# A graph layer on one core: where W_self's first rows are loaded, and in what order its first products run

## The chip, the cores and the metric

The kernel runs on one core of a Trainium2 chip. The metric is the device time of one execution in microseconds; lower is better. The core has five engines that run their own instruction streams and meet only at semaphores: TensorE (PE in the profile), VectorE (DVE), ScalarE (ACT), GpSimd (POOL) and SyncE (SP). Loads and stores are DMAs, which SP and ACT issue here.

## The reference

The inputs are 625 nodes of 512 features, 20625 edges with four relations and a weight each, and the weights of the layer. Cut to what matters:

```
h   = relu(layernorm(x))
agg = segment_sum over edges of (h[src] @ W_rel[type] + b_rel[type]) * weight   # by dst
agg = agg / max(sum of the weights by dst, 1)
x1  = layernorm(h + h @ W_self + b_self + agg) * g1 + b1
ffn = gelu(x1 @ W1 + b_ffn1) @ W2 + b_ffn2
out = x + layernorm(x1 + ffn) * g2 + b2
```

The change touches only the first lines: the normalized rows h and their product with W_self (512 x 512).

## The kernel before

The 625 nodes are five row tiles of 125 rows, numbered 0 to 4 (in the trace all of them are `x`, in the built program `x_60`). All float32 products are made of three products of a rounded part ("high", type fp32r) and what is left ("low"): high by high, low by high and high by low. Each operand must therefore be split: ScalarE casts the high part, then VectorE subtracts it from the original to get the low part.

The start of the program, tile by tile, is a relay between three engines:

- `row_mean(c)` on VectorE waits for tile c of x, takes its statistics and writes the negated mean (lines 629, 633, 634).
- `h_of(c)` on ScalarE subtracts the mean and clamps at zero (line 506). The scale of the layer norm is applied later.
- `turn_h(c)` on TensorE transposes the tile in four pieces (line 1033).
- `hT_high(c)` on ScalarE casts the transposed tile's high part (line 511), and `hT_low(c)` on VectorE makes its low part (line 638).

W_self comes as two units of 256 rows; a unit is two halves of 128 rows (k = 0 and 1). Unit 0's halves are two DMAs of 256 KB with signals of their own. `first_high(0)` and `first_high(1)` (lines 498 and 501) cast them, and two subtractions (lines 651 and 656) make their low parts; the signals are `first_hi` and `w_hi`, `first_lo` and `w_lo`. Unit 1 is one DMA of 512 KB, split by `high_part(1)` (line 492, ScalarE) and `low_part(1)` (line 625, VectorE).

On TensorE `first_product(k, s)` multiplies row tile s by half k of unit 0, high by high and low by high; `product_lo` adds high by low; `unit_product(u, s)` is all six products of unit u and tile s. Ten and then three dummy products of ones, 128 x 128 each, fill time before the first real product.

Nothing schedules this at run time. Every engine takes its instructions strictly in the order in which the code of that engine is written, so an instruction that waits holds back all that stand behind it. The order of SP's DMAs is also that of the code: three tiles of x (112 of each tile's rows; ScalarE's queue loads the 13 rows that are left over), then W_self's two first halves, then two tiles of x, unit 1, the edge lists, and the rest. After the self product come the four relations' products (units 2 to 9), the products that pick the edges' fields (`pick`), the building of the adjacency blocks and their products, and the two feed-forward layers.

Of the kernel before, what the change touches and what calls it, by code (L numbers as in the profile page):

```python
# [19 lines left out]
def gnn_layer(nc, x, src, dst, etype, ew, W_self, b_self, W_rel, b_rel, ln1_g, ln1_b, ln2_g, ln2_b,  # L20
# [156 lines left out]
    with ctx:  # L177
# [112 lines left out]
        def stage_view(u):  # L290
            v = stage[u % STAGES][:, :]
            return v if U_REL <= u < U_W1 else v.rearrange("p (k n) -> p k n", k=2)
# [59 lines left out]
        @block.sync  # L352
        def _(sp):

            def load_x(c):
                p0, p1 = SPANS[0]
                sp.dma_start(x1[p0:p1, c, :], x[c * TN + p0:c * TN + p1, :]).then_inc(x_in[c], 16)  # L357

            def load(u):
                if u >= STAGES:  # L360
                    sp.wait_ge(w_lo, u - STAGES + 1)
                sp.dma_start(stage_view(u), units[u][0]).then_inc(stage_in[u % STAGES], 16)

            def sums_by_relation(c):

                sp.wait_ge(A_a, group_of(c, NG - 1))
                sp.wait_ge(A_b, group_of(c, NG - 1))
                if c >= 2:
                    sp.wait_ge(agg_ps, c - 1)
                for row, half in zip(SUM_ROWS, (0, 1, 0)):  # L370
                    sp.dma_start(f32(sums[row:row + TR, c % 2, :]),
                                 f32(AT[c % 2][half][SUMS:SUMS + 1, :, :])).then_inc(sums_in[c % 2], 16)

            for c in range(3):
                load_x(c)
            sp.dma_start(stage_view(0)[:, 0, :], units[0][0][:, 0, :]).then_inc(first_in, 16)
            sp.dma_start(stage_view(0)[:, 1, :], units[0][0][:, 1, :]).then_inc(stage_in[0], 16)
            for c in range(3, NT):
                load_x(c)
            load(1)  # L380
            sp.wait_ge(tails, 1)
            for f, vec, signal in ((1, dst, dst_in), (3, ew.bitcast(I32), w_in), (0, src, src_in), (2, etype, src_in)):
                flat = vec.rearrange("(p e) -> p e", p=TN)
                sp.dma_start(raw[0:TN, f, 0:EC], flat).then_inc(signal, 16)
                sp.dma_start(raw[0:TN - 1, f, EC:EW], flat[1:TN, 0:EW - EC]).then_inc(signal, 16)
            load(2)
            for buf, vec in ((bself_bc, b_self), (g1_bc, ln1_g), (b1_bc, ln1_b)):
                row = vec.rearrange("(a d) -> a d", a=1)
                sp.dma_start(buf[:, :], row.broadcast_to([P, D])).then_inc(consts_in, 16)
            with nc.allow_non_contiguous_dma("bias by partition"):  # L390
                sp.dma_start(bf1, b1.rearrange("(f p) -> p f", p=P)).then_inc(consts_in, 16)
            sp.wait_ge(blk_iotas, 3)
            for row in SUM_ROWS:
                for r in range(R):
                    sp.dma_start(brel_raw[row + r * NT:row + (r + 1) * NT, :],
                                 b_rel[r:r + 1, :].broadcast_to([NT, D])).then_inc(brel_in, 16)
            for u in range(STAGES, U_REL):
                load(u)
            sums_by_relation(0)
            for u in range(U_REL, U_REL + STAGES):  # L400
                load(u)
            for c in range(1, NT):
                sums_by_relation(c)
            for u in range(U_REL + STAGES, NU):
                load(u)

            sp.wait_ge(agg_ps, NT)
            for c in range(NT):
                for p0, p1 in SPANS:
                    sp.dma_start(x_again[p0:p1, c, :], x[c * TN + p0:c * TN + p1, :]).then_inc(late_in, 16)  # L410
            for buf, vec in ((g2_bc, ln2_g), (b2_bc, ln2_b), (bf2_bc, b2)):
                row = vec.rearrange("(a d) -> a d", a=1)
                sp.dma_start(buf[:, :], row.broadcast_to([P, D])).then_inc(late_in, 16)
            for c in range(NT - 1):
                sp.wait_ge(y_out, c + 1)
                for p0, p1 in SPANS:
                    sp.dma_start(out[c * TN + p0:c * TN + p1, :], ybuf[p0:p1, c % 2, :]).then_inc(out_done[c % 2], 16)
            p0, p1 = SPANS[0]
            for i, (d0, d1) in enumerate(HALVES):
                sp.wait_ge(y_out, NT + i)  # L420
                sp.dma_start(out[(NT - 1) * TN + p0:(NT - 1) * TN + p1, d0:d1],
                             ybuf[p0:p1, (NT - 1) % 2, d0:d1]).then_inc(last_done, 16)
            for i in range(2):
                sp.wait_ge(out_done[i], ROWS_IN * len(range(i, NT - 1, 2)))
            sp.wait_ge(last_done, 16 * 2 * len(HALVES))
# [52 lines left out]
        def _(act):  # L478
# [24 lines left out]
            def h_of(c):  # L503

                act.wait_ge(xmean, c + 1)
                a.activation(x1[0:TN, c, :], x1[0:TN, c, :], ACT.Relu,
                             bias=nm[0:TN, c:c + 1]).then_inc(h_act, 1)

            def hT_high(c):
                act.wait_ge(hT_ps, c + 1)  # L510
                a.copy(hT_all[:, :, 0, :, c, :],
                       h_bank(c).rearrange("p (h k m) -> p h k m", h=2, k=2)[:, :, :, 0:TN]).then_inc(hT_a, 1)
# [25 lines left out]
            a.activation(nm1, ones[:, 0:1], ACT.Relu).then_inc(table_in, 1)  # L538

            h_of(0)  # L540
            h_of(1)
            hT_high(0)
            first_high(0)
            hT_high(1)
            first_high(1)
            h_of(2)
            hT_high(2)
            h_of(3)
            hT_high(3)
            h_of(4)  # L550
            hT_high(4)
            high_part(1)
            act.wait_ge(dst_in, 16 * 2)
            a.copy(DF[0:TN, 1, 0:EW], raw[0:TN, 1, :]).then_inc(dsts, 1)
            high_part(2)
# [58 lines left out]
        def _(dve):  # L614
# [21 lines left out]
            def hT_low(c):  # L636
# [8 lines left out]

            row_mean(0)
            row_mean(1)
            row_mean(2)
            hT_low(0)
            dve.wait_ge(first_hi, 1)  # L650
            v.tensor_tensor(units[0][2][:, 0, :], stage_view(0)[:, 0, :], f32(units[0][1][:, 0, :]),
                            ALU.subtract).then_inc(first_lo, 1)
            hT_low(1)
            row_mean(3)
            dve.wait_ge(w_hi, 1)
            v.tensor_tensor(units[0][2][:, 1, :], stage_view(0)[:, 1, :], f32(units[0][1][:, 1, :]),
                            ALU.subtract).then_inc(w_lo, 1)
            hT_low(2)
            row_mean(4)
            hT_low(3)  # L660
            hT_low(4)
            dve.wait_ge(dst_in, 16 * 2)
            link(v.tensor_copy(edge_d, raw[0:TN, 1, 0:ES * (EG + 1)].rearrange("p (j e) -> p j e", e=ES)[:, :, 0]))
# [1 line left out]
            dve.wait_ge(w_in, 16 * 2)  # L665
            v.tensor_reduce(wmax, raw[0:TN, 3, 0:EC].bitcast(F32), AX.X, ALU.max,
                            apply_absolute_value=True).then_inc(wmax_in, 1)
            low_part(1)
            dve.wait_ge(iotas, 1)
            for j in range(EG + 1):  # L670
                i = v.tensor_scalar(ahead[0:TN, j, :], slot_d[0:TN, :], edge_d[:, j:j + 1], None, ALU.is_gt)
# [352 lines left out]
        def _(pe):  # L1024
# [30 lines left out]
            def product_lo(u, s):  # L1055

                half, w = u % 2, wring[:, u % WRING, :, :, :]
                if s == 0:
                    pe.wait_ge(w_lo, u + 1)
                if s == 0 and u == 0:  # L1060
                    pe.wait_ge(first_lo, 1)
                for k in range(2):
                    i = mm(ps[0:TN, s, :], hT_all[:, half, 0, k, s, :], w[:, 1, k, :], False, half == 1 and k == 1)
                return i

            def unit_product(u, s):
                product_hi(u, s)
                return product_lo(u, s)

            def first_product(k, s):  # L1070

                if s == 0 and k == 0:
                    pe.wait_ge(first_hi, 1)
                if s == 0 and k == 1:
                    pe.wait_ge(w_hi, 1)
                if k == 0:
                    pe.wait_ge(hT_a, s + 1)
                mm(ps[0:TN, s, :], hT_all[:, 0, 0, k, s, :], wring[:, 0, 0, k, :], k == 0)
                if k == 0:
                    pe.wait_ge(hT_b, s + 1)  # L1080
                mm(ps[0:TN, s, :], hT_all[:, 0, 1, k, s, :], wring[:, 0, 0, k, :], False)
# [89 lines left out]
            dummies(WARM[0])  # L1171
            pe.wait_ge(blk_iotas, 2)
            turn_h(0)
            turn_h(1)
            dummies(WARM[1])
            first_product(0, 0)
            first_product(1, 0)
            turn_h(2)
            first_product(0, 1)
            first_product(1, 1)  # L1180
            product_lo(0, 0)
            turn_h(3)
            product_lo(0, 1)
            unit_product(0, 2)
            turn_h(4)
            unit_product(0, 3)
            unit_product(0, 4).then_inc(unit_done, 1)
            unit_product(1, 0).then_inc(self_ps, 1)
            unit_product(1, 1).then_inc(self_ps, 1)

            pe.wait_ge(wmax_in, 1)
            mm(WSUM, ones[0:TN, :], wmax, True, True).then_inc(wsum_ps, 1)
# [169 lines left out]
```

## Time and profile before

| | |
|---|---|
| median of 3 timed runs | 242.24 us (242.18 to 242.71) |
| the profiled execution | 242.38 us |
| its span in the trace | 240.6 us |
| PE busy | 232.5 us, 97% of the span |
| DVE busy | 180.8 us, 75% |
| ACT busy | 65.7 us, 27% |
| PE busy from 5.33 to 8.85 us | 2.58 of 3.52 us |
| PE busy from 8.85 to 14.34 us | 5.49 of 5.49 us |

TensorE is busy nearly all the time; what it isn't lies mostly ahead of 8.85 us and behind 235 us. A time that is lost or won at the start is therefore lost or won at the end, unless something between holds TensorE up.

### The profile page before, as it was taken

To read this page: it belongs to the slowest core of one execution; us is meant where nothing else is said; L and a number is where in the kernel's file an instruction comes from. 1 tells how busy PE (TensorE), PEld (TensorE's weight loads), DVE (VectorE), ACT (ScalarE), POOL (GpSimd) and SP (SyncE) were. 2 spreads that over 40 slices of the span, in tenths; PEclk is the share of its full clock that TensorE was granted. 3 is DMA by queue.
4 is the path that set the end of the run, shared out by engine and by line. 5 is a ranking of instruction groups with operands and counts; after the bars stand their busy time and mean duration, and the time that the engine had idled before them with its cause. 6 is when DMAs were issued, how large, how long until landed. Compare 5 with 4: busy or idle time off the path is not lost.

```text
span 240.6 us, 4100 instructions
## 1 busy us (share of the span) xinstructions
PE 232.5 (97%) x1691; PEld 192.8 (80%) x1691; DVE 180.8 (75%) x339; ACT 65.7 (27%) x87; POOL 16.6 (7%) x36
## 2 busy tenths in 40 slices
PE   7999999999999999999999999999999999999990
PEld 7688787777787777877877877887899999887890
DVE  3969679799987868778799698739439789655564
ACT  3761434156062052102102202403316533100000
POOL 8020000000000000000010020002000000011111
PEclk9999999999999999999999999999999999999997
DMA  7788700223005200000000000005600860011111
GB/s 197 232 221 164 235 17 9 86 66 114 0 5 179 87 0 3 1 7 1 3 7 0 0 8 0 3 5 154 198 0 0 251 184 1 0 28 60 43 43 43
DMA packets 10392, 15.95 MB, mean 66 GB/s; under 512 B 2946, under 2 KB 3696, under 8 KB 10370
## 3 DMA queue, kind: packets, MB, share of 16 engines
q1 hardware_dynamic: 10188, 15.49, 22.9%
q8 instruction: 15, 0.25, 0.4%
q10 hardware_dynamic: 182, 0.16, 0.2%
q14 instruction: 7, 0.06, 0.1%
HBM read 14.22 MB, written 1.28 MB: 64 GB/s over the span
## 4 chain that ended last, share of the span: by engine, by line
PE 83%; DVE 8%; issue 4%; DMA 2%; ACT 1%; SPq 1%; POOL 0%; POOLq 0%; DVEq 0%
PE ps L1026 82%; DMA stage<-in_L_gnn_W_self 2%; DVE T_lo L797 1%; DVE eqp L725 1%; PE ps L1129 1%; DVE kw L737 1%; PE ps L1033 1%; SPq L357 1%; DVE wring L625 0%; DVE keq L732 0%; POOL small L475 0%; DVE pairs L713 0%; DVE pairs L710 0%; DVE pairs L716 0%; DVE small L1010 0%
## 5 line engine op out<-in xcount | busy, mean ns | idle before, releaser
L1026 PE MATMUL ps<-wring,hT 128*125 128x512 f32 x300 | 73.1, 398 | 0.4 <-ACT wring L501 0.3
L1026 PEld LDWEIGHTS ps<-wring,hT 128*125 128x125 f32 x300 | 54.5, 185 | 13.8 <-ACT wring L501 0.6
L1026 PE MATMUL ps<-T_hi,AT_hi 125*125 125x512 f32 x100 | 40.3, 403 | 0.0
L1026 PE MATMUL ps<-T_lo,AT_hi 125*125 125x512 f32 x100 | 39.4, 394 | 0.0
L725 DVE TENSOR_TENSOR eqp<-iota_p,pairs 128x1638 f16<-128x1638 f16 x25 | 25.1, 1005 | 2.8 <-issue 1.5
L1026 PE MATMUL ps<-T_hi,AT_lo 125*125 125x512 f32 x100 | 26.0, 403 | 0.0
L529 ACT CAST AT_hi<-ps 128x1500 fp32r<-128x1500 f32 (+1 forms) x10 | 12.3, 1234 | 48.8 <-PE ps L1026 48.6
L1026 PEld LDWEIGHTS ps<-kw,eqp 128*128 128x128 f16 x650 | 19.5, 97 | 6.4 <-issue 6.0
L1026 PE MATMUL ps<-kw,eqp 128*128 128x40 f16 (+1 forms) x650 | 21.9, 190 | 0.2 <-DVE kw L737 0.2
L1026 PEld LDWEIGHTS ps<-T_lo,AT_hi 125*125 125x125 f32 x100 | 18.6, 186 | 4.2
L1026 PEld LDWEIGHTS ps<-T_hi,AT_hi 125*125 125x125 f32 x100 | 18.5, 185 | 4.2
L790 DVE TENSOR_TENSOR AT_lo<-ps,AT_hi 128x1500 fp32r<-128x1500 f32 (+1 forms) x10 | 14.6, 1458 | 8.7 <-ACT AT_hi L529 8.7
L1026 PEld LDWEIGHTS ps<-T_hi,AT_lo 125*125 125x125 f32 x100 | 17.7, 185 | 3.8
L737 DVE TENSOR_TENSOR kw<-keq,pairs 128x520 f16<-128x520 f16 x50 | 19.2, 425 | 0.9
L518 ACT ACTIVATE T_hi<-ps,small 125x512 fp32r<-125x512 f32 x20 | 13.8, 689 | 21.3 <-PE ps L1026 21.2
L1026 PE MATMUL ps<-x1T_hi,W_hi 128*128 128x378 f32 (+1 forms) x64 | 18.9, 310 | 0.0
L1026 PE MATMUL ps<-x1T_lo,W_hi 128*128 128x378 f32 (+1 forms) x64 | 18.7, 308 | 0.0
L1026 PE MATMUL ps<-W_hi,u_lo 128*125 128x512 f32 (+2 forms) x48 | 17.5, 364 | 0.0
L1026 PE MATMUL ps<-W_hi,u_hi 128*125 128x512 f32 (+2 forms) x48 | 17.5, 364 | 0.0
L1026 PE MATMUL ps<-W_lo,u_hi 128*125 128x512 f32 (+2 forms) x48 | 17.5, 364 | 0.0
L797 DVE SCALAR_TENSOR_TENSOR T_lo<-ps,small,T_hi 125x512 fp32r<-125x512 f32 x20 | 14.3, 747 | 4.2 <-ACT T_hi L518 4.2
L470 POOL TENSOR_TENSOR small<-small 125x1 f32<-125x1 f32 x5 | 5.0, 1003 | 160.3 <-DVE small L825 160.3
(129 smaller groups left out, 277.8 us busy)
## 6 DMA issues: line engine op xcount, KB each, us to landing
stage<-in_L_gnn_W_rel SPq DMA_DIRECT2D x8, 512.0 KB, 3.8
stage<-in_L_gnn_W_ffn SPq DMA_DIRECT2D x8, 512.0 KB, 4.1
x<-in_x SPq DMA_DIRECT2D x5, 224.0 KB
x_again<-in_x SPq DMA_DIRECT2D x5, 224.0 KB
out<-ybuf SPq DMA_DIRECT2D x4, 224.0 KB
stage<-in_L_gnn_W_self SPq DMA_DIRECT2D x2, 256.0 KB, 5.3
stage<-in_L_gnn_W_self SPq DMA_DIRECT2D x1, 512.0 KB, 6.8
g_bc<-in_L_gnn_ln_g SPq DMA_DIRECT2D x2, 256.0 KB, 6.3
```

The costliest lines, as they stand in the source:

```text
L357: sp.dma_start(x1[p0:p1, c, :], x[c * TN + p0:c * TN + p1, :]).then_inc(x_in[c], 16)
L470: g.tensor_tensor(rs1[0:TN, c:c + 1], ve1[0:TN, c:c + 1], mhalf[0:TN, 0:1], ALU.pow).then_inc(ln1_r, 1)
L518: a.mul(T_hi[0:TN, r, s, :], ps[0:TN, s, :], rstd[0:TN, s:s + 1]).then_inc(T_a, 1)
L529: a.copy(AT[n % 2][0][:, :, i0 * BW:(i0 + nb) * BW].rearrange("p q (i d) -> p i q d", i=nb), A_banks(g)[:, :, 0:TR * BW].rearrange("p i (q ...
L725: v.tensor_tensor(eqp[0:EK, z, :, 0:OW].rearrange("e s (n z) -> e s n z", z=2), iota_p[0:EK, 0:OW].rearrange("e (n z) -> e n z", z=2).unsq ...
L737: i = v.tensor_tensor(kw[0:EK, z, part, :, :, :], keq[0:EK, :, :, :], pairs[0:EK, 2 + part, at, :].unsqueeze(2).broadcast_to([EK, SL, TR, ...
L790: v.tensor_tensor(lo[:, :, cols].rearrange("p q (i d) -> p i q d", i=nb), A_banks(g)[:, :, 0:TR * BW].rearrange("p i (q d) -> p i q d", q=TR),
L797: v.scalar_tensor_tensor(out=T_lo[0:TN, r, s, :], in0=ps[0:TN, s, :], scalar=rstd[0:TN, s:s + 1], in1=f32(T_hi[0:TN, r, s, :]), op0=ALU.mu ...
L1026: return nc.tensor.matmul(o, l, r, start=start, stop=stop, skip_group_check=True)
L1033: i = nc.tensor.transpose(h_bank(c)[:, k * P:k * P + TN], x1[0:TN, c, k * P:(k + 1) * P], ident[0:TN, 0:TN])
L1129: i = nc.tensor.transpose(TURN[:, k * P:k * P + TN], x1[0:TN, c, k * P:(k + 1) * P], ident[0:TN, 0:TN])
```

## The change

It has four parts. On SP, W_self's first half is issued behind tile 0 of x, and its second half behind tile 1, where both stood behind tile 2. On ScalarE, `first_high(k)` stands ahead of `hT_high(k)`, each tile's clamp, half and turned tile follow one another, and `high_part(1)` goes ahead of `hT_high(4)`. On VectorE, the low part of half 0 stands ahead of `hT_low(0)` and both ahead of `row_mean(2)`; the low part of half 1 goes ahead of `row_mean(3)`; `low_part(1)` goes ahead of `hT_low(4)`. On TensorE, `first_product` is cut into `high_high`, `high_low` and `low_high`, which are mixed with the transposes, and unit 1's high products of tiles 0 and 1 stand ahead of unit 0's product of tile 4. No instruction is added or taken away.

```diff
-            for c in range(3):
-                load_x(c)
+            load_x(0)
             sp.dma_start(stage_view(0)[:, 0, :], units[0][0][:, 0, :]).then_inc(first_in, 16)
+            load_x(1)
             sp.dma_start(stage_view(0)[:, 1, :], units[0][0][:, 1, :]).then_inc(stage_in[0], 16)
-            for c in range(3, NT):
+            for c in range(2, NT):
                 load_x(c)
...
             h_of(0)
+            first_high(0)
+            hT_high(0)
             h_of(1)
-            hT_high(0)
-            first_high(0)
+            first_high(1)
             hT_high(1)
-            first_high(1)
...
             h_of(4)
+            high_part(1)
             hT_high(4)
-            high_part(1)
...
-            def first_product(k, s):
+            def high_high(k, s):
 
                 if s == 0 and k == 0:
                     pe.wait_ge(first_hi, 1)
...
                 if k == 0:
                     pe.wait_ge(hT_a, s + 1)
                 mm(ps[0:TN, s, :], hT_all[:, 0, 0, k, s, :], wring[:, 0, 0, k, :], k == 0)
+
+            def high_low(k, s):
+                if s == 0 and k == 0:
+                    pe.wait_ge(first_lo, 1)
+                if s == 0 and k == 1:
+                    pe.wait_ge(w_lo, 1)
+                mm(ps[0:TN, s, :], hT_all[:, 0, 0, k, s, :], wring[:, 0, 1, k, :], False)
+
+            def low_high(k, s):
                 if k == 0:
                     pe.wait_ge(hT_b, s + 1)
                 mm(ps[0:TN, s, :], hT_all[:, 0, 1, k, s, :], wring[:, 0, 0, k, :], False)
```

How the change moves instructions on VectorE, from the mean of tile 1 on. The rows are those of the built program: line, operation, what is written from what, shape, and the semaphores waited for. BN_STATS to TENSOR_SCALAR is one `row_mean`, `hT` one `hT_low`, `wring` the low part of a half of W_self. Before:

```order
L629 BN_STATS small<-x_60 125x6 [waits x_in1]
L633 BN_AGGR small<-small 125x2 [waits dchain]
L634 TENSOR_SCALAR small<-small 125x1 [waits dchain]
L629 BN_STATS small<-x_60 125x6 [waits x_in2]
L633 BN_AGGR small<-small 125x2 [waits dchain]
L634 TENSOR_SCALAR small<-small 125x1 [waits dchain]
L638 TENSOR_TENSOR hT<-ps,hT 128x2x2x125 [waits hT_a]
L651 TENSOR_TENSOR wring<-stage_52,wring 128x512 [waits first_hi]
L638 TENSOR_TENSOR hT<-ps,hT 128x2x2x125 [waits hT_a]
L629 BN_STATS small<-x_60 125x6 [waits x_in3]
```

The same place with the change:

```order
L629 BN_STATS small<-x_60 125x6 [waits x_in1]
L633 BN_AGGR small<-small 125x2 [waits dchain]
L634 TENSOR_SCALAR small<-small 125x1 [waits dchain]
L649 TENSOR_TENSOR wring<-stage_52,wring 128x512 [waits first_hi]
L638 TENSOR_TENSOR hT<-ps,hT 128x2x2x125 [waits hT_a]
L629 BN_STATS small<-x_60 125x6 [waits x_in2]
L633 BN_AGGR small<-small 125x2 [waits dchain]
L634 TENSOR_SCALAR small<-small 125x1 [waits dchain]
L638 TENSOR_TENSOR hT<-ps,hT 128x2x2x125 [waits hT_a]
L655 TENSOR_TENSOR wring<-stage_52,wring 128x512 [waits w_hi]
```

The two low parts and `hT_low(0)` have moved up past the means of tiles 2 and 3, and all of them stand behind the mean of tile 1.

On TensorE, from the first dummies to tile 4. Rows on `ones` are dummies, rows on `ident,x_60` transposes (four to a tile), rows on `wring,hT` products with W_self. Before:

```order
L1026 MATMUL ps<-ones 128x128 x10
L1033 MATMUL ps<-ident,x_60 128x125 x8
L1026 MATMUL ps<-ones 128x128 x3
L1026 MATMUL ps<-wring,hT 125x512 x4
L1033 MATMUL ps<-ident,x_60 128x125 x4
L1026 MATMUL ps<-wring,hT 125x512 x6
L1033 MATMUL ps<-ident,x_60 128x125 x4
L1026 MATMUL ps<-wring,hT 125x512 x8
L1033 MATMUL ps<-ident,x_60 128x125 x4
L1026 MATMUL ps<-wring,hT 125x512 x24
```

The same place with the change:

```order
L1033 MATMUL ps<-ident,x_60 128x125 x4
L1026 MATMUL ps<-ones 128x128 x3
L1026 MATMUL ps<-wring,hT 125x512 x2
L1033 MATMUL ps<-ident,x_60 128x125 x4
L1026 MATMUL ps<-wring,hT 125x512 x5
L1033 MATMUL ps<-ident,x_60 128x125 x4
L1026 MATMUL ps<-wring,hT 125x512 x5
L1033 MATMUL ps<-ident,x_60 128x125 x4
L1026 MATMUL ps<-wring,hT 125x512 x6
L1033 MATMUL ps<-ident,x_60 128x125 x4
L1026 MATMUL ps<-wring,hT 125x512 x24
```

Two products now stand between the transposes of tiles 0 and 1, and 2, 7 and 12 products ahead of the transposes of tiles 1, 2 and 3 (before 0, 4 and 10). Ahead of tile 4's stand 18, as before, and 24 behind it.

On ScalarE, from the first clamp on. L506 is `h_of`, L511 `hT_high`, L498 and L501 are the two halves of `first_high`. Before:

```order
L506 ACTIVATE x_60<-x_60,small 125x512 [waits xmean] x2
L511 CAST hT<-ps 128x2x2x125 [waits hT_ps]
L498 CAST wring<-stage_52 128x512 [waits first_in]
L511 CAST hT<-ps 128x2x2x125 [waits hT_ps]
L501 CAST wring<-stage_52 128x512 [waits stage_in0]
L506 ACTIVATE x_60<-x_60,small 125x512 [waits xmean]
```

The same place with the change:

```order
L506 ACTIVATE x_60<-x_60,small 125x512 [waits xmean]
L498 CAST wring<-stage_52 128x512 [waits first_in]
L511 CAST hT<-ps 128x2x2x125 [waits hT_ps]
L506 ACTIVATE x_60<-x_60,small 125x512 [waits xmean]
L501 CAST wring<-stage_52 128x512 [waits stage_in0]
L511 CAST hT<-ps 128x2x2x125 [waits hT_ps]
```

The clamp of tile 1 now stands behind the cast of W_self's first half and that of turned tile 0.

## Rows read from the trace of the kernel before

**Rows 1.** Busy time of the engines by stretch, us from the span's start
```profile
core 0: us, PE busy (x) PEld busy (x) DVE busy (x) ACT busy (x) POOL busy (x), PEclk, DMA share, GB/s
5.33:8.85 3.52, 2.58 (x18) 1.92 (x17) 2.87 (x9) 3.08 (x7) 0.88 (x2) 1.00 1.06 302
8.85:14.34 5.49, 5.49 (x29) 4.15 (x30) 4.14 (x10) 2.96 (x5) 1.45 (x2) 1.00 0.58 163
```

**Rows 2.** Chain of work that ended last: start us, us, what
```profile
2.09 5.06 DMA stage<-in_L_gnn_W_self
...
7.18 0.62 ACT wring L498
```

**Rows 3.** TensorE in order of time: start us, us, engine, line, operation, tiles, count
```profile
0.97 4.36 PE L1026 MATMUL ps<-ones 128*128 128x128 f32 x20 [0.97 <-POOL ones L438]
5.70 0.62 PE L1033 MATMUL ps<-ident,x 125*128 125x125 f32 x4 [0.37 <-ACT x L506]
...
7.10 0.84 PE L1026 MATMUL ps<-ones 128*128 128x128 f32 x6
7.85 0.72 PE L1026 MATMUL ps<-wring,hT 128*125 128x512 f32 x2
8.85 0.73 PE L1026 MATMUL ps<-wring,hT 128*125 128x512 f32 x2 [0.27 <-ACT wring L501]
...
11.42 0.63 PE L1033 MATMUL ps<-ident,x 125*128 125x125 f32 x4
11.81 2.10 PE L1026 MATMUL ps<-wring,hT 128*125 128x512 f32 x8
13.75 0.59 PE L1033 MATMUL ps<-ident,x 125*128 125x125 f32 x4
14.10 5.82 PE L1026 MATMUL ps<-wring,hT 128*125 128x512 f32 x24
```

**Rows 4.** VectorE in order of time, from the mean of tile 1
```profile
4.72 0.68 DVE L629 BATCH_NORM_STATS2 small<-x 125x6 f32<-125x512 f32 x1
...
6.32 0.69 DVE L629 BATCH_NORM_STATS2 small<-x 125x6 f32<-125x512 f32 x1 [0.51 <-DMA x<-in_x]
...
7.33 0.67 DVE L638 TENSOR_TENSOR hT<-ps,hT 128x500 fp32r<-128x500 f32 x1
7.92 0.68 DVE L651 TENSOR_TENSOR wring<-stage,wring 128x512 fp32r<-128x512 f32 x1
8.52 0.67 DVE L638 TENSOR_TENSOR hT<-ps,hT 128x500 fp32r<-128x500 f32 x1
...
10.04 0.15 DVE L634 TENSOR_SCALAR small<-small 125x1 f32<-125x1 f32 x1
...
12.29 0.15 DVE L634 TENSOR_SCALAR small<-small 125x1 f32<-125x1 f32 x1
```

**Rows 5.** ScalarE in order of time, the casts and clamps that are named
```profile
6.47 0.56 ACT L511 CAST hT<-ps 128x500 fp32r<-128x500 f32 x1
...
10.63 0.72 ACT L506 ACTIVATE x<-x,small 125x512 f32<-125x512 f32 x1
12.09 0.58 ACT L511 CAST hT<-ps 128x500 fp32r<-128x500 f32 x1 [0.74 <-PE ps L1033]
12.56 0.73 ACT L506 ACTIVATE x<-x,small 125x512 f32<-125x512 f32 x1
```

**Rows 6.** DMAs issued up to 30 us: KB each, median us to landing
```profile
stage<-in_L_gnn_W_self SPq DMA_DIRECT2D x2, 256.0 KB, 5.3
```

**Rows 7.** The DMA queues from 1.5 to 8.1 us
```profile
DMA packets 1053, 1.81 MB, mean 274 GB/s; under 512 B 169, under 2 KB 169, under 8 KB 1053
```

**Rows 8.** What stands ahead of the picks, VectorE and TensorE in order of time
```profile
23.91 0.48 DVE L694 SCALAR_TENSOR_TENSOR DF<-raw,small,DF 125x260 f16<-125x260 f32 x1
28.35 2.99 PE L1026 MATMUL ps<-chosen,DF 125*128 125x325 f16 x25
```

More of the change, by code:

```diff
@@ L647, in _ @@
             row_mean(1)
-            row_mean(2)
-            hT_low(0)
             dve.wait_ge(first_hi, 1)
@@ L652, in _ @@
                             ALU.subtract).then_inc(first_lo, 1)
+            hT_low(0)
+            row_mean(2)
             hT_low(1)
-            row_mean(3)
             dve.wait_ge(w_hi, 1)
@@ L657, in _ @@
                             ALU.subtract).then_inc(w_lo, 1)
+            row_mean(3)
             hT_low(2)
@@ L660, in _ @@
             hT_low(3)
+            low_part(1)
             hT_low(4)
@@ L667, in _ @@
                             apply_absolute_value=True).then_inc(wmax_in, 1)
-            low_part(1)
             dve.wait_ge(iotas, 1)
@@ L1059, in product_lo @@
                     pe.wait_ge(w_lo, u + 1)
-                if s == 0 and u == 0:
-                    pe.wait_ge(first_lo, 1)
                 for k in range(2):
@@ L1173, in _ @@
             turn_h(0)
+            dummies(WARM[1])
+            high_high(0, 0)
+            high_low(0, 0)
             turn_h(1)
-            dummies(WARM[1])
-            first_product(0, 0)
-            first_product(1, 0)
-            turn_h(2)
-            first_product(0, 1)
-            first_product(1, 1)
-            product_lo(0, 0)
+            low_high(0, 0)
+            high_high(1, 0)
+            low_high(1, 0)
+            high_high(0, 1)
+            high_low(0, 1)
+            turn_h(2)
+            low_high(0, 1)
+            high_high(1, 1)
+            low_high(1, 1)
+            high_low(1, 0)
+            high_low(1, 1)
             turn_h(3)
-            product_lo(0, 1)
             unit_product(0, 2)
@@ L1186, in _ @@
             unit_product(0, 3)
+            product_hi(1, 0)
+            product_hi(1, 1)
             unit_product(0, 4).then_inc(unit_done, 1)
-            unit_product(1, 0).then_inc(self_ps, 1)
-            unit_product(1, 1).then_inc(self_ps, 1)
+            product_lo(1, 0).then_inc(self_ps, 1)
+            product_lo(1, 1).then_inc(self_ps, 1)
             pe.wait_ge(wmax_in, 1)
```

## The prediction

> **What bounds the kernel now.** I read the busy time by stretch first [rows 1]: from 8.85 to 14.34 us TensorE is busy 5.49 of 5.49 us, while from 5.33 to 8.85 it is busy only 2.58 of 3.52. So everything that starts behind 8.85 is paced by TensorE's own work, and the start is where time can be won: 0.94 us of idle time, and 0.84 us of dummies that fill a wait [rows 3].
>
> Then the chain that ended last [rows 2]: it goes through the DMA of W_self's first half, issued at 2.09 and landed 5.06 us later at 7.16, and its cast at 7.18. The first product starts at 7.85 [rows 3]. The turned tile 0 was cast already at 6.47 to 7.03 [rows 5]; that is how long the first product would have to wait if the half were early.
>
> Then VectorE [rows 4]. It has 0.51 us of idle time ahead of tile 2's statistics, ended by a DMA: tile 2 lands at 6.3. From there to the last mean, written at 12.44, its rows follow one another without a wait. Tile 4's clamp starts at 12.56 and ends at 13.29 [rows 5], and tile 4's transposes start at 13.75, when TensorE gets to them [rows 3]. So VectorE and ScalarE's relay is only 0.4 us ahead of TensorE. That is the row on which my forecast rests: whatever delays the means by more than 0.4 us is paid by TensorE.
>
> **The change part by part.** No instruction is added, so the sum is the shift of the moment from which TensorE has no gap again. Ahead of tile 4's transposes stand 18 products in both programs and behind them 24 in both. The 24 start at 14.10 now [rows 3]; I work out where they start with the change.
>
> *Landings.* W_self's first half moves from the fourth place of SP's queue to the second, its second half from fifth to fourth, tile 1 of x from second to third, tile 2 from third to fifth. Tile 1 had landed by 4.72, where its statistics start with no wait; the third place landed at 6.3 [rows 4], the fourth at 7.16 [rows 2], the fifth at about 8.0 (the two halves took 5.3 in the median, the first 5.06, so the second some 5.5 from about 2.5) [rows 2, 6]. The size of a place hardly matters (112 or 128 rows of 2 KB). I read the new landings by place: first half under 5 us, tile 1 at 6.3, second half at 7.16, tile 2 at 8.0. The other reading is by size: the half puts 262 KB ahead of tile 1, which at the 274 GB/s of that stretch [rows 7] is 0.96 us; tile 1 would land at about 5.6. I take the place, because the third place shows a step (at least 1.6 us behind the second, where the fourth came 0.86 behind the third), and the load that stood there had no more bytes than the one ahead of it. Both stay in the range.
>
> The Trainium skill, "DMA: Bandwidth & Descriptors", Specifications, gives some 27 GiB/s for each of the 16 DMA engines. From that figure 262 KB take an estimated 0.57 us, tile 1 would land at 5.3, and the sum below would shrink to about +0.2 us; the trace's 274 GB/s lies well under that figure, and the measurement decides.
>
> *VectorE.* `row_mean(1)` now waits for tile 1: idle from 4.8 to 6.3, where it waited 0.51 us. Behind it on the same queue stand the low part of half 0, although its cast is ready by about 6.1, `hT_low(0)` and all later means. Steps by the spacing of the rows [rows 4]: a mean 1.01 us, 1.08 until it is written (6.32 to 7.33 and 7.41), a low part 0.59 or 0.60. From 6.32: mean 1 written 7.41; low part of half 0 from 7.33; `hT_low(0)` 7.93; mean 2 8.52 to 9.60; `hT_low(1)` 9.53; low part of half 1 10.12; mean 3 from 10.73, written 11.81. Now it is written at 10.19 [rows 4].
>
> *The relay of the last two tiles.* Clamp of tile 3 11.84 to 12.56 (0.72), transposes from 12.62 (0.06 to 0.15 behind a clamp), 0.63 long, until 13.25, `hT_high(3)` at 13.29, the next of ScalarE 0.47 later [rows 3, 5]: clamp of tile 4 13.76 to 14.49. Mean 4 is written at about 13.4 and isn't late. Transposes of tile 4 14.55, first product 0.35 behind them (13.75 to 14.10): **14.90 in place of 14.10, +0.80 us**.
>
> *TensorE meanwhile.* The first product starts at about 7.05 instead of 7.85, and so 0.8 us is won there. It is given back in waits: the high-by-low product waits for VectorE until 8.0, tile 1's transposes for the clamp until 8.25 (now 6.62), tile 2's until 10.4 (now 9.47), tile 3's until 12.6 (now 11.42 [rows 3]). The 18 products are work of 4.2 us (24 take 5.82 to the end of the last, 0.235 apart); they all fit in the gaps.
>
> *Costed at nothing.* `high_part(1)` ahead of `hT_high(4)` and `low_part(1)` ahead of `hT_low(4)`: tile 4's low part comes at about 17.3, and TensorE gets to its first use at about 18.7, 14 products behind 14.90 and then two more, since unit 1's eight high products now stand ahead. Without that cover it would wait some 0.4 us. Further on the picks start at 28.35, and the last VectorE result that they need starts at 23.91 and takes 0.48 [rows 8]: 4 us of slack, and both move together. Half 1's low part is ready when it is needed. So I find nothing ahead of the picks that takes the shift up, nor behind them, where TensorE is busy and all loads come by its progress.
>
> The sum: 242.38 + 0.80 = 243.18 for the profiled execution, 0.14 above the median; against the median 242.24 it is **243.05 us**.
>
> **The rivals.** A measurement of this kernel tells about 0.2% (0.48 us) from no change.
>
> *Tile 1 lands by size, not by place* (5.6 or earlier): the means are written 0.7 us earlier than above, mean 3 at about 11.15, tile 4's transposes at 13.9: +0.15 us, 242.4. VectorE is then held by the turned tiles as much as by x, so that a still earlier landing gives nothing more. For it speaks the rate [rows 7]; against it the step at the third place. Chance 0.21.
>
> *Faster: the early first product carries through.* The first half's landing is on the chain [rows 2], and without it the first product could start 0.8 us earlier. That needs mean 3 written before 10.0, so that tiles 3 and 4 don't hold TensorE. From 4.72 VectorE has 7.2 us of work to the last mean (12.44 less 4.72 less 0.51), so it could be written at 11.95, 0.5 us earlier; worth about 0.6 us: 241.65. It decides if tile 1 lands by about 4.8 with the half ahead of it, and if no low part waits for ScalarE. Chance 0.08.
>
> *The change doesn't bring the half forward:* it lands at about 7 all the same. Then its cast, which now stands ahead of `hT_high(0)` and the clamp of tile 1 on ScalarE, holds the whole relay: clamp of tile 1 at 8.2 instead of 5.84, some +1.5 us, 243.8. The first load shows that 230 KB can be there early. Chance 0.06.
>
> *TensorE's clock falls.* The granted clock is 1.00 in both stretches [rows 1], the 2.4 GHz level. The twenty dummy passes at the start came 0.21 us apart, the later six 0.11 [rows 3], so half speed doubles a product. With the change TensorE idles about 2.3 us between 5.3 and 14.6, in pieces under 0.7. If it ran at the 1.2 GHz level from 8 to 15 us, the 18 products and the transposes would cost 5.5 us more, of which the gaps take some 2: +3.5, 245.7. Behind this sentence stands the Trainium skill, "TensorE: Matmul & The Clock Gate", which ties the clock to recent activity; no run here shows how short the gaps must be. Chance 0.05.
>
> **How the numbers follow.** The forecast (tile 1 between 5.95 and 6.8) has 0.60, with its own range of 242.75 to 243.5, since each us of tile 1's landing is one us of the end. Range: from 242.2, which leaves out the faster case, to 243.9, which takes in the late half and leaves out the clock. Slower by over 0.2%: the forecast less a little that ends under +0.48, the half, the clock: 0.68. Within: 0.24. Faster: 0.08.
>
> **What would show it.** In the profile of the changed kernel: first product at about 7.05; an idle time of some 1.5 us ahead of VectorE's second statistics, ended by the DMA of x, at 6.3; mean 3 written at 11.8; waits of TensorE ahead of the transposes of tiles 1 to 3; the run of 24 products from 14.9; no longer wait at the picks; granted clock 1.00. The prediction is wrong if tile 1 is there before 5.9, or if the 24 products start at 14.9 and the end doesn't move.

## The result and the profile after

The changed kernel takes 243.63 us in the median of 19 runs (242.50 to 244.12), the kernel before 242.68 us in 19 runs on the same chips (242.01 to 243.45). The ratio is 1.0037, with a 95% interval of 1.0025 to 1.0048: slower by some 0.9 us. The forecast was 0.8 us slower.

The profiled execution took 243.91 us, its span is 242.1 us, 1.5 us over the span before. Only two of the 19 runs were slower. TensorE's part of the trace, in order of time (start us, us, engine, line, operation, tiles, count; in brackets the idle time ahead and what ended it), which answers to [rows 3]:

```profile
5.55 0.62 PE L1033 MATMUL ps<-ident,x 125*128 125x125 f32 x4 [0.24 <-ACT x L506]
6.01 0.84 PE L1026 MATMUL ps<-ones 128*128 128x128 f32 x6
6.93 0.46 PE L1026 MATMUL ps<-wring,hT 128*125 128x512 f32 x1
8.68 0.50 PE L1026 MATMUL ps<-wring,hT 128*125 128x512 f32 x1 [1.28 <-DVE wring L649]
9.01 0.59 PE L1033 MATMUL ps<-ident,x 125*128 125x125 f32 x4
9.36 1.64 PE L1026 MATMUL ps<-wring,hT 128*125 128x512 f32 x5
11.03 0.65 PE L1033 MATMUL ps<-ident,x 125*128 125x125 f32 x4
11.43 1.41 PE L1026 MATMUL ps<-wring,hT 128*125 128x512 f32 x5
13.34 0.65 PE L1033 MATMUL ps<-ident,x 125*128 125x125 f32 x4 [0.50 <-ACT x L506]
13.75 1.64 PE L1026 MATMUL ps<-wring,hT 128*125 128x512 f32 x6
15.28 0.65 PE L1033 MATMUL ps<-ident,x 125*128 125x125 f32 x4
15.68 4.67 PE L1026 MATMUL ps<-wring,hT 128*125 128x512 f32 x19
```

The first product starts at 6.93, 0.92 us earlier than before. The second then waits 1.28 us for the low part of W_self's first half (L649, VectorE), and the row of 24 products behind tile 4's transposes (the view ends at 20 us and shows 19 of them), which began at 14.10, begins at 15.68.

VectorE shows why its low part is late, although the half was cast long before; this answers to [rows 4]:

```profile
4.50 0.15 DVE L634 TENSOR_SCALAR small<-small 125x1 f32<-125x1 f32 x1
6.92 0.69 DVE L629 BATCH_NORM_STATS2 small<-x 125x6 f32<-125x512 f32 x1 [2.27 <-DMA x<-in_x]
7.65 0.18 DVE L633 BATCH_NORM_AGGREGATE small<-small 125x2 f32<-125x6 f32 x1
7.87 0.15 DVE L634 TENSOR_SCALAR small<-small 125x1 f32<-125x1 f32 x1
7.94 0.68 DVE L649 TENSOR_TENSOR wring<-stage,wring 128x512 fp32r<-128x512 f32 x1
8.54 0.67 DVE L638 TENSOR_TENSOR hT<-ps,hT 128x500 fp32r<-128x500 f32 x1
...
12.38 0.15 DVE L634 TENSOR_SCALAR small<-small 125x1 f32<-125x1 f32 x1
```

Tile 1's statistics start at 6.92 instead of 4.72, behind 2.27 us of idle time that ends with the DMA of x. Everything behind them waits too. The mean of tile 3 is written at 12.53, before at 10.19. ScalarE:

```profile
5.32 0.60 ACT L498 CAST wring<-stage 128x512 fp32r<-128x512 f32 x1
6.21 0.58 ACT L511 CAST hT<-ps 128x500 fp32r<-128x500 f32 x1 [0.29 <-PE ps L1033]
8.05 0.72 ACT L506 ACTIVATE x<-x,small 125x512 f32<-125x512 f32 x1 [1.27 <-DVE small L634]
...
12.57 0.72 ACT L506 ACTIVATE x<-x,small 125x512 f32<-125x512 f32 x1 [0.28 <-DVE small L634]
14.03 0.58 ACT L511 CAST hT<-ps 128x500 fp32r<-128x500 f32 x1 [0.73 <-PE ps L1033]
14.50 0.72 ACT L506 ACTIVATE x<-x,small 125x512 f32<-125x512 f32 x1
```

The half is cast at 5.32 (before 7.18), right behind tile 0's clamp: the first half did come early. The clamps of tiles 1 and 3 wait for their means, 1.27 and 0.28 us; that of tile 4 stands behind the cast of turned tile 3 and starts at 14.50 (before 12.56). In the chain that ended last, the DMA of tile 1 has taken the place of the DMA of W_self's first half [rows 2]:

```profile
1.62 5.28 DMA x<-in_x
6.90 0.02 issue
6.92 0.70 DVE small L629
```

Behind the start nothing takes the shift up. TensorE later on, where the picks (f16) stood at 28.35 before [rows 8]:

```profile
21.48 8.61 PE L1026 MATMUL ps<-wring,hT 128*125 128x512 f32 x36
29.94 2.99 PE L1026 MATMUL ps<-chosen,DF 125*128 125x325 f16 x25
```

They come at 29.94, 1.59 us later, with no wait ahead of them, and the span is 1.5 us longer.

### The profile page after: what moved, and what is told of

Read it like the earlier page. It is cut to its first block, busy times and chain, and to the rows that moved or that the text cites. A ratio compares the mean times of both kernels' runs of the same rounds, so it can differ in the third digit from the quotient of the medians.

```text
span 242.1 us, 4099 instructions
## 1 busy us (share of the span) xinstructions
PE 232.7 (96%) x1691; PEld 192.6 (80%) x1691; DVE 180.9 (75%) x339; ACT 65.9 (27%) x87; POOL 16.6 (7%) x36
## 3 DMA queue, kind: packets, MB, share of 16 engines
HBM read 14.22 MB, written 1.28 MB: 64 GB/s over the span
## 4 chain that ended last, share of the span: by engine, by line
PE 89%; issue 3%; DVE 3%; DMA 2%; ACT 1%; POOL 0%; SPq 0%; POOLq 0%; DVEq 0%
PE ps L1026 88%; DMA x<-in_x 2%; PE ps L1136 1%; PE ps L1033 1%; DVE small L629 1%; POOL small L475 0%; ACT x L506 0%; DVE small L1010 0%; DVE t2buf L1009 0%; DVE hT L638 0%; POOLq L177 0%; DVE ybuf L1002 0%; DVE wring L649 0%; DVE wring L655 0%; ACT hT L511 0%
```

## The experiments

Two theories stood against each other from the start. A: the relay of VectorE, ScalarE and TensorE is held by whichever load it meets late, in the change tile 1 of x. B: the new, finer order of the engines costs the time. Four kernels went first. All are timed beside the kernel before, which took 242.80 us on the chip of these four and 242.63 on the chip of the four that follow.

**The queue's order alone (e1).** The engines keep the orders of before:

```diff
-            for c in range(3):
-                load_x(c)
+            load_x(0)
             sp.dma_start(stage_view(0)[:, 0, :], units[0][0][:, 0, :]).then_inc(first_in, 16)
+            load_x(1)
             sp.dma_start(stage_view(0)[:, 1, :], units[0][0][:, 1, :]).then_inc(stage_in[0], 16)
-            for c in range(3, NT):
+            for c in range(2, NT):
                 load_x(c)
```

> The engines' orders of before with the change's order of SP's DMAs. Theory A (tile 1's late landing holds VectorE and with it the relay): tile 1 lands at about 6.3 to 6.9, and since here tile 2's mean also stands directly behind tile 1's, and tile 2 lands at about 8.0, all low parts wait for tile 2; the steps of the rows give tile 4's transposes at 15.3, some +1.6 us (243.9 to 244.4, ratio 1.006 to 1.008), more than the change itself. Theory B (the time is lost in the new orders of the engines, the queue's order is harmless or a gain): no slower than before, 242.0 to 242.9.

Measured: 244.76 us (244.04 to 246.32, 6 runs), ratio 1.0086 (1.0057 to 1.0114). Theory A, and more than twice the loss of the change. It is also more than theory A had worked out (243.9 to 244.4): two of the six runs took 246.3 us at a lower clock, which e7 below takes up. VectorE of this kernel now waits for tile 2 as well:

```profile
6.87 0.69 DVE L629 BATCH_NORM_STATS2 small<-x 125x6 f32<-125x512 f32 x1 [2.26 <-DMA x<-in_x]
...
8.64 0.70 DVE L629 BATCH_NORM_STATS2 small<-x 125x6 f32<-125x512 f32 x1 [0.67 <-DMA x<-in_x]
```

So the queue's order alone does harm, and with the new orders of the engines on top the loss is half as large.

**The engines' orders alone (e2).** SP's DMAs are those of before, all else is the changed kernel (the diff above, the other way round, applied to it).

> The engines' orders of the change with SP's DMAs in the order of before. Theory A: tile 1 is there by 4.7, but W_self's first half lands at 7.2, and ScalarE casts it ahead of turned tile 0 and tile 1's clamp; the relay starts late for another reason, tile 1's clamp at about 8.2, and the steps of the rows give some +1.5 us, ratio 1.005 to 1.007. If instead only the queue's order costs time (theory C: the engines' orders are harmless): ratio 1.000.

Measured: 244.33 us (243.92 to 245.73, 6 runs), ratio 1.0075 (1.0049 to 1.0100). Theory A; C fell. Here it is ScalarE that waits:

```profile
7.48 0.62 ACT L498 CAST wring<-stage 128x512 fp32r<-128x512 f32 x1 [2.23 <-DMA stage<-in_L_gnn_W_self]
8.01 0.57 ACT L511 CAST hT<-ps 128x500 fp32r<-128x500 f32 x1
8.48 0.72 ACT L506 ACTIVATE x<-x,small 125x512 f32<-125x512 f32 x1
```

Tile 1 was there in time, and its mean too, but its clamp stands behind the cast of a half that lands at 7.46: 8.48 in place of 5.84. Each of the two parts of the change is worse alone than both together. Two of the six runs (244.94 and 245.73 us) have a mean clock of 0.988 and 0.983, under the 0.990 to 0.996 of the kernel before; the other four, at 0.991 or more, took 243.9 to 244.4 us and are still 1.1 us or more over before.

**Is it the place in the queue or the bytes ahead (e3)?** The forecast read tile 1's landing from its place. In the kernel before, tile 0's load was cut in two:

```diff
-            for c in range(3):
+            for p0, p1 in ((0, 48), (48, SPANS[0][1])):
+                sp.dma_start(x1[p0:p1, 0, :], x[p0:p1, :]).then_inc(x_in[0], 16)
+            for c in range(1, 3):
                 load_x(c)
...
-                dve.wait_ge(x_in[c], ROWS_IN)
+                dve.wait_ge(x_in[c], ROWS_IN + 16 * (c == 0))
```

> The kernel before, with tile 0's load of 112 rows cut into two DMAs of 48 and 64 rows, so that tile 1 stands third in SP's queue with no more bytes ahead of it than before. If a load lands by its place (theory P): tile 1 lands at 5.7 to 6.5 where it landed by 4.7, W_self's first half at about 8.0, and the time grows by 0.7 to 1.0 us. If it lands by the bytes ahead of it (theory S): tile 1 within 0.5 us of 4.7 (SP's issue of one more DMA takes 0.45), the first half at 7.2 to 7.6, the time up by 0 to 0.4 us.

Measured: 243.08 us (242.49 to 244.12, 12 runs), ratio 1.0013 (1.0000 to 1.0027). VectorE's statistics of tiles 0, 1 and 2:

```profile
3.92 0.69 DVE L631 BATCH_NORM_STATS2 small<-x 125x6 f32<-125x512 f32 x1 [2.81 <-DMA x<-in_x]
...
5.02 0.69 DVE L631 BATCH_NORM_STATS2 small<-x 125x6 f32<-125x512 f32 x1
...
6.04 0.68 DVE L631 BATCH_NORM_STATS2 small<-x 125x6 f32<-125x512 f32 x1
```

Tile 1 stands third in the queue and its statistics start at 5.02, tile 2 stands fourth and is there by 6.04. So the place does nothing of the kind that the forecast took (a step of 1.6 us): theory S. Behind the same bytes, tile 2 landed at 6.3, 6.7, 6.0 and 6.4 us in the profiled executions of the kernel before, e2, e3 and w1, and tile 1 of the changed kernels has nearly the same bytes ahead of it. The split isn't quite free in this execution: ScalarE waits for W_self's second half until 8.9 (before, it landed at 8.05), and TensorE 0.67 us for its cast.

**The change's last part undone (e4).** Unit 1's cast, low part and high products go back to where they were:

```diff
             h_of(4)
-            high_part(1)
             hT_high(4)
+            high_part(1)
...
-            product_hi(1, 0)
-            product_hi(1, 1)
             unit_product(0, 4).then_inc(unit_done, 1)
-            product_lo(1, 0).then_inc(self_ps, 1)
-            product_lo(1, 1).then_inc(self_ps, 1)
+            unit_product(1, 0).then_inc(self_ps, 1)
+            unit_product(1, 1).then_inc(self_ps, 1)
```

> The changed kernel with its last part undone: unit 1's casts, its low part and its high products of tiles 0 and 1 stand where they stood before. Theory A: that part is hidden either way (TensorE gets to tile 4's low part 0.4 us or more behind its end), so the time is that of the changed kernel, ratio to before 1.003 to 1.005. If the reordered tail costs time (theory T: low_part(1) ahead of hT_low(4) makes TensorE wait): 0.2 us or more faster than the changed kernel, ratio about 1.002.

Measured: 243.66 us (242.77 to 243.90, 10 runs), ratio 1.0039 (1.0028 to 1.0051): theory A, and T (1.002) fell. That part is worth nothing that these runs can tell. Its profiled execution took 242.77 us and is useful in another way, since tile 1 landed earlier in it than in that of the changed kernel. VectorE:

```profile
6.00 0.69 DVE L629 BATCH_NORM_STATS2 small<-x 125x6 f32<-125x512 f32 x1 [1.20 <-DMA x<-in_x]
```

and TensorE:

```profile
14.76 5.80 PE L1026 MATMUL ps<-wring,hT 128*125 128x512 f32 x24
```

The statistics of tile 1 are 0.92 us earlier (6.00 against 6.92), the row of products behind tile 4 is 0.92 us earlier (14.76 against 15.68), and the execution is 1.1 us shorter. Up to this row the two kernels are alike, so in these two executions tile 1's landing passes to TensorE one to one.

Four more kernels followed: two on what is left when data are in time, one on the clock and one from what was found.

**Tile 1 on time, tile 2 late (e5).** The changed kernel with both halves issued between tiles 1 and 2 (`load_x(0)`, `load_x(1)`, the two halves, the rest).

> The changed kernel with SP's DMAs in the order tile 0, tile 1, first half, second half, tile 2: tile 1 is on time again, the first half third in the queue (about 6.3), tile 2 fifth as in the change. Theory A (the relay of all engines is held by whichever load it meets late): ScalarE's cast of the half at 6.3 stands ahead of tile 1's clamp, and the steps of the rows give +0.7 us over before (ratio about 1.003), close to the change itself. Theory D (tile 1's landing alone is the whole loss): about 0.2 us over before, ratio 1.001 or less.

Measured: 243.64 us (243.03 to 244.38, 6 runs), ratio 1.0038 (1.0026 to 1.0051). Theory A; D fell: it isn't tile 1 as such. The half was expected at 6.3 and came at 7.45 in this execution, the slowest of the six, so that the size is borne out by the median alone. ScalarE waits for the half until 7.47, and the clamp of tile 1 behind it starts at 8.46:

```profile
7.47 0.62 ACT L498 CAST wring<-stage 128x512 fp32r<-128x512 f32 x1 [2.08 <-DMA stage<-in_L_gnn_W_self]
7.99 0.57 ACT L511 CAST hT<-ps 128x500 fp32r<-128x500 f32 x1
8.46 0.72 ACT L506 ACTIVATE x<-x,small 125x512 f32<-125x512 f32 x1
```

**No load of the first half (e6).** The changed kernel leaves out the DMA of W_self's first 128 rows and takes zeros for them:

```diff
-            sp.dma_start(stage_view(0)[:, 0, :], units[0][0][:, 0, :]).then_inc(first_in, 16)
...
+            g.memset(stage_view(0)[:, 0, :], 0.0).then_inc(first_in, 1)
             g.memset(mhalf, -0.5)
...
-                    act.wait_ge(first_in, 16)
+                    act.wait_ge(first_in, 1)
```

> The changed kernel without the DMA of W_self's first half (its 128 rows are set to zero by GpSimd instead of being loaded), so that the half is early and nothing stands ahead of tile 1. Theory A: tile 1 lands by 4.7, VectorE's wait of 1.2 to 2.3 us is gone, and what is left are the new engine orders with all data in time: within 0.3 us of the kernel before (ratio 0.999 to 1.001), 0.6 to 0.9 us faster than the changed kernel. Theory B (the finer mixing on ScalarE and TensorE costs the time): still 0.6 us or more over before. Theory G (mixing gains when its data are there): 0.5 us or more faster than before.

Measured: 242.70 us (242.20 to 243.02, 11 runs) beside 242.63 of before, ratio 0.9999 (0.9990 to 1.0008). Theory A to the letter; B fell, and so did G. Without the 262 KB ahead of tile 1 the whole 0.9 us is gone. Tile 1's statistics start at 4.68, with no wait for it. The queue is lighter for tile 2 too, which lands at 7.6 in place of 8.7, but VectorE waits for it by at most 0.1 us in either kernel. TensorE:

```profile
6.96 0.69 PE L1026 MATMUL ps<-wring,hT 128*125 128x512 f32 x2
...
11.87 0.65 PE L1033 MATMUL ps<-ident,x 125*128 125x125 f32 x4 [0.57 <-ACT x L506]
...
14.21 5.82 PE L1026 MATMUL ps<-wring,hT 128*125 128x512 f32 x24
```

The first product starts 0.9 us earlier than before, and nothing comes of it: at tile 3's transposes TensorE waits 0.57 us for the clamp, and the 24 products start at 14.21, before at 14.10. Even with its data in time, the new order wins nothing, since the means set the pace: the low parts of W_self now stand ahead of tile 3's mean, which is written at 11.06 (before 10.19).

**The clock in the first experiment (e7).** Its profile holds something that the steps don't give. Busy time by stretch (the column behind POOL is the granted clock), the kernel with the queue's order alone:

```profile
7.72:14.55 6.83, 5.77 (x21) 5.07 (x22) 4.76 (x13) 4.23 (x8) 0.00 (x0) 0.50 0.63 166
```

The granted clock is 0.50 for 6.8 us, the 1.2 GHz level. It falls at 7.72, 1.6 us into an idle time of TensorE of 2.65 us:

```profile
5.51 0.62 PE L1033 MATMUL ps<-ident,x 125*128 125x125 f32 x4 [0.47 <-ACT x L506]
8.78 1.09 PE L1033 MATMUL ps<-ident,x 125*128 125x125 f32 x4 [2.65 <-ACT x L506]
```

So eleven dummy products were put into that gap:

```diff
             turn_h(0)
+            dummies(11)
             turn_h(1)
```

> The kernel e1_queue_only with eleven more dummy products between the transposes of tiles 0 and 1, where TensorE idled 2.65 us. They fit in the gap (some 2.4 us at half speed, 1.2 at full). In e1's profile the granted clock fell to 0.5 of full speed at 7.7 us, for 6.8 us. If that fall is due to the gap (theory H), the clock stays at 1.00 here, and the time is 0.3 to 1.0 us below e1's 244.76, about 243.9 to 244.4, as the steps alone gave. If the fall is not due to the gap: as e1, 244.5 to 245.

Measured: 244.56 us (244.14 to 244.74, 5 runs), ratio 1.0079 (1.0065 to 1.0092). The same stretch of this kernel:

```profile
7.72:14.55 6.83, 6.67 (x44) 5.21 (x43) 5.74 (x14) 4.78 (x9) 0.00 (x0) 1.00 0.63 171
```

Without the dummies two of six runs took 246.3 us, at a mean clock of 0.976 and 0.977; the other four 244.0 to 244.9. With them none of five is over 244.74 and the mean clock is 0.991 or more in each. So the clock did what theory H says, and the time did not: H had 243.9 to 244.4, the other theory 244.5 to 245, and the medians differ by only 0.2 us. Five runs against six don't prove that the gap is what lets the clock fall. In the two executions of e1 that show the fall most clearly it goes with some 2 us (246.3 against 244.0 to 244.9). Two more runs of e1, 244.64 and 244.89, have a mean clock of 0.983, so the clock may have fallen for a shorter time there too. The dummies were longer than expected: their 22 passes took 2.4 us and not 1.2 at the full clock, and tile 1's transposes start at 9.05, 0.55 us behind the end of the clamp.

**A version from what was found (w1).** In the kernel before, TensorE waits until 8.85 for the cast of W_self's second half. Two products that are ready can go there. Only TensorE's order changes (`first(a, b, k, s)` is one product: a and b are 1 for the low part of h and of W; further down the products that are left follow in the places between the transposes):

```diff
-            first_product(0, 0)
-            first_product(1, 0)
+            first(0, 0, 0, 0)
+            first(1, 0, 0, 0)
+            first(0, 0, 0, 1)
+            first(0, 1, 0, 0)
+            first(0, 0, 1, 0)
+            first(1, 0, 1, 0)
             turn_h(2)
...
```

> The kernel before with only TensorE's order changed: the high-by-high product of tile 1 and the high-by-low product of tile 0 with the first half move into the wait for the second half's cast (8.3 to 8.8 us), where TensorE idled 0.27 us and more. Two products of 0.235 us fit; tile 4's clamp ends 0.4 us ahead of its transposes, which bounds the gain. The steps give -0.23 us, ratio 0.999; if TensorE's waits for the turned tiles are what binds, 1.000.

Measured: 242.37 us (242.00 to 242.82, 11 runs) beside 242.63, ratio 0.9991 (0.9982 to 1.0000). The gap between the first products is gone, and the 24 products start at 14.00:

```profile
7.98 1.76 PE L1026 MATMUL ps<-wring,hT 128*125 128x512 f32 x6
...
14.00 5.81 PE L1026 MATMUL ps<-wring,hT 128*125 128x512 f32 x24
```

By the medians that is the size that the steps gave (-0.23 us), but at the edge of what the runs can tell from nothing, and in the profiled execution the 24 products moved by only 0.10 us. The gain is not shown.

## Why the prediction was right, step by step

- *What bounds the start.* Right: the relay of means, clamps and turned tiles was 0.4 us ahead of TensorE, and a delay beyond that is paid in full. The changed kernel and e4 show it one to one over 0.92 us, and e6 shows the loss gone with the load that caused it.
- *The first half comes early and the first product with it.* Right: forecast 7.05, measured 6.93. So was its being given back in waits (1.28 us for the low part, 0.50 ahead of tile 3).
- *Tile 1's landing, 6.3.* It landed at 6.9 in the profiled execution, and at 6.9, 6.0 and 6.6 in those of e1, e4 and e7; where it landed in the timed runs was not seen. The reason given for 6.3 did not hold: the split load shows that the place in the queue is nothing. The rival reading, bytes at 274 GB/s, was right in kind but gave too early a landing (5.6). The trace shows where it fails. Of tile 1's 30 recorded increments of its semaphore, the 22nd came at 4.4 us in the kernel before and at 4.8 to 5.1 in the changed kernel, e1 and e4 (5.6 in e7): in three of the four less than the 0.96 us that the bytes at 274 GB/s explain. But the last one, for which VectorE waits, came at 4.6 before and at 6.0 to 6.9 with the half ahead. In the changed kernel 28 had come by 5.52 us and the last two at 6.60 and 6.90; in the others the last ones trail off more evenly. A mean rate doesn't tell of that. In the kernel before, tile 2, with nearly the same bytes in and ahead of it, landed at 6.3. The landing was thus read from the row next to it in bytes, and it was luck that this row was next to it in place too. Why the last increments come so late was not tried.
- *W_self's second half (forecast 7.16) and tile 2 (8.0).* Both were read by place, and landed at 8.05 and 8.7. Neither held an engine up: ScalarE got to the half at 8.68 and VectorE to the tile at 9.12.
- *The size.* Predicted +0.80, measured +0.9 (ratio 1.0037). So close a hit is in part luck. Against the profile of before the 24 products start 1.58 us later in the changed kernel's profiled execution, with tile 1 at 6.9, and 0.66 us later in e4's, with tile 1 at 6.0. The steps themselves come out 0.2 us short: with tile 1 at 6.9 they put the 24 products 0.6 us behind the forecast's 14.90, at 15.5, and they started at 15.68. Of that, 0.12 us is VectorE's `hT_low(1)`, which waited for ScalarE's cast of turned tile 1 until 10.22, and 0.05 the step from tile 4's transposes to the product behind them (0.40, taken as 0.35). The forecast's about +0.2 for a landing at 5.3 doesn't fit its +0.15 for one at 5.6; neither landing came about.
- *Costed at nothing.* Right: unit 1's part is hidden (e4), and nothing up to the picks or behind takes the shift up.
- *The rivals.* Faster: the early first product doesn't carry through even with tile 1 on time (e6, ratio 0.9999). This rival wanted tile 3's mean written before 10.0, but the forecast's own steps take 5.5 us from tile 1's statistics to that mean (6.32 to 11.81), so that from 4.72 it is written at 10.2 at the earliest; by these steps the rival was out of reach. The late half did not come about in the change, but e2 is that case: +1.5 us was worked out, and 1.5 us measured by the medians (244.33 less 242.80), 1.8 by the ratio, some of it with a lower clock. The clock did not fall in the changed kernel (granted 1.00 from 5.33 to 20 us, with a longest gap of 1.28 us where the forecast had under 0.7), but did in e1, in a gap of 2.65 us.

## What to carry to other kernels

A load that is moved forward in a queue is paid by those that it passes: look what waits for them, and what stands behind that wait on its engine, before counting what the moved load wins. Where several engines hand tiles to one another in a fixed order, work out when the last tile gets through; a product that starts earlier than the relay can follow is given back in waits. When loads are crowded, read a landing from a row with the same bytes ahead of it, and not from a mean rate; even so it can be off by as much as the executions differ, here 0.9 us.

## What the runs showed of the hardware

- The same load lands at quite different times from one execution to the next: tile 1 at 6.9, 6.9, 6.0 and 6.6 us in the four profiled executions that have the half ahead of it (the changed kernel, e1, e4, e7). The changed kernel's 19 runs spread over 1.6 us, but those of the kernel before, where tile 1 is on time, over 1.4 us too; how much of it comes from landings was not measured.
- In e1's profiled execution the granted clock fell to half for 6.8 us, 1.6 us into a gap of 2.65 us in TensorE's work; with gaps of 2.03 us (e2), 1.78 us (e5) and 1.28 us (the changed kernel) it did not fall in the profiled executions. It differs from run to run: two of e1's six runs took 246.3 us at a mean clock of 0.976 and 0.977, two have 0.993 and 0.994, and one of e2's six has 0.983. The Trainium skill, "TensorE: Matmul & The Clock Gate", Part 1: The HAM clock gate, says that the clock falls after TensorE has been idle, and that the point of a transition varies because it depends on a phase that doesn't start with the kernel. That the same kernel shows the fall in some runs and not in others agrees, but would also fit gaps that differ with the landings, which were seen in the profiled executions alone.
